# Row sums that come with the adds, squares on ScalarE, and the second FFN's add in two places: a macaron block on one core

## What is computed

```python
x1 = x  + 0.5 * ffn(layernorm(x))           # ffn: one 256x256 matrix, a weighted sum of 8 adapters, and a bias
y  = layernorm(x1)                          # input of the attention block
h  = layernorm(y, ln1_g, ln1_b)             # time-mixed with its predecessor token: xk, xv, xr
ya = y + (sigmoid(xr @ Wr.T) * wkv(xk @ Wk.T, xv @ Wv.T)) @ Wo.T
h  = layernorm(ya, ln2_g, ln2_b)            # mixed again: xck, xcr
kk = square(relu(xck @ Wck.T))
x2 = x1 + ya + sigmoid(xcr @ Wcr.T) * (kk @ Wcv.T)
out = x2 + 0.5 * ffn(layernorm(x2))
# layernorm: m = mean(x), v = mean((x - m)**2), (x - m) / sqrt(v + 1e-5), over the 256 channels
```

## Time and profile before

| | us |
|---|---|
| median of 3 runs (435.98 to 436.53) | 436.53 |
| the profiled execution | 435.98 |
| its span, first to last instruction | 434.2 |
| TensorE's matmuls busy | 419.3 |
| VectorE busy | 380.5 |
| ScalarE busy | 305.9 |
| GpSimd busy | 179.1 |

### The profile page before, as it was taken

The page is one execution under the profiler, slowest core; times in us unless marked ns, Lnnn a source line. Parts: engine busy times, 40 slices in busy tenths (PEclk is TensorE's granted clock), DMA queues, the critical chain, the costliest instruction groups (busy, mean ns, idle before and its releaser), DMA issues. The chain is left out here.

```text
span 434.2 us, 6241 instructions
## 1 busy us (share of the span) xinstructions
PE 419.3 (97%) x2042; PEld 336.1 (77%) x2042; DVE 380.5 (88%) x779; ACT 305.9 (70%) x573; POOL 179.1 (41%) x164
## 2 busy tenths in 40 slices
PE   8989988989999999999999999999999999999996
PEld 8855865668868887798769886888779876988985
DVE  3989989999999999999999999999999999976235
ACT  1158977896689677994789668967797478945420
POOL 1545053626281646344462728154643346033011
PEclk9999999999999999999999999999999999999998
DMA  6991010001000200011000200010001000000101
GB/s 209 385 396 54 2 48 0 2 2 51 0 0 2 97 2 1 0 51 48 2 0 26 74 0 2 0 51 0 2 0 49 2 0 2 30 19 1 49 2 49
DMA packets 15971, 18.52 MB, mean 43 GB/s; under 512 B 1082, under 2 KB 13634, under 8 KB 15938
## 3 DMA queue, kind: packets, MB, share of 16 engines
q1 hardware_dynamic: 14538, 17.05, 11.1%
q10 hardware_dynamic: 1400, 1.07, 0.8%
HBM read 13.92 MB, written 4.19 MB: 42 GB/s over the span
## 5 line engine op out<-in xcount | busy, mean ns | idle before, releaser
L477 PE MATMUL pair<-wcv_sb,kk 128*128 128x256 f32 x448 | 100.4, 380 | 0.0
L477 PEld LDWEIGHTS pair<-wcv_sb,kk 128*128 128x128 f32 x448 | 83.8, 190 | 11.3 <-ACT kk L717 0.6
L1282 POOL TENSOR_TENSOR x2b<-xs,bias_bc 128x512 f32<-128x512 f32 (+1 forms) x16 | 20.1, 1256 | 92.4 <-DVE xs L1100 48.6
L451 PE MATMUL pair<-xck_hi,wck_hi 128*128 128x512 f32 x128 | 54.3, 424 | 0.0
L455 PE MATMUL pair<-xck_lo,wck_hi 128*128 128x512 f32 x128 | 50.6, 395 | 0.0
L452 PE MATMUL pair<-xck_hi,wck_lo 128*128 128x512 f32 x128 | 50.6, 395 | 0.0
L713 ACT ACTIVATE kk<-pair 128x512 f32<-128x512 f32 x64 | 36.4, 591 | 20.0 <-PE pair L455 19.8
L1282 POOL TENSOR_TENSOR x<-x,bias_bc 128x512 f32<-128x512 f32 x14 | 18.1, 1295 | 63.4 <-DVE rwkv L1016 36.3
L1322 POOL TENSOR_TENSOR xs<-x,xa 128x512 f32<-128x512 f32 x16 | 20.4, 1274 | 44.9 <-DVE xa L1022 44.3
L717 ACT ACTIVATE kk<-kk 128x512 f32<-128x512 f32 x64 | 35.9, 626 | 0.0
L1262 POOL TENSOR_TENSOR rstd_x<-vare_x,nhalf 128x4 f32<-128x4 f32 (+2 forms) x26 | 30.1, 1157 | 8.9 <-DVE vare_x L876 7.4
(11 more groups left out here) (159 smaller groups left out, 1069.3 us busy)
## 6 DMA issues: line engine op xcount, KB each, us to landing
x<-in_x_dram SPq DMA_DIRECT2D x8, 512.0 KB, 3.5
out_dram<-xs SPq DMA_DIRECT2D x15, 256.0 KB, 2.1
xt<-in_xt_dram SPq DMA_DIRECT2D x4, 512.0 KB, 7.5
work<-in_ffn_w_dram ACTq DMA_DIRECT2D x4, 256.0 KB, 4.1
work<-in_ffn_w_dram SPq DMA_DIRECT2D x4, 256.0 KB, 4.3
kk<-in_wck_dram SPq DMA_DIRECT2D x1, 1024.0 KB, 10.1
xs<-in_xt_dram SPq DMA_DIRECT2D x2, 512.0 KB, 11.2
wcv_sb<-in_wcv_dram SPq DMA_DIRECT2D x1, 1024.0 KB, 12.9
```

The lines of the kernel that those rows point to most:

```text
L451: nc.tensor.matmul(key_bank(n), wck_hi[:, h, cols], xck_hi[:, h, :], start=h == 0, stop=False)
L477: last = nc.tensor.matmul(bank_of("kv", e, i)[:, t % TB * C:(t % TB + 1) * C], kk[:, n, tok:tok + P], wcv_sb[:, n, :], start=n == 0, stop= ...
L1282: nc.gpsimd.tensor_tensor(dst, tile, bias_bc[:, :].rearrange("p (a c) -> p a c", a=1).broadcast_to([P, tiles, C]), ALU.add).then_inc(done, 1)
```

## The change

Items 0 to 5 (`SUMS_X2`) take x2's statistics, and items from 2 on (`SUMS_X1`) x1's, without bn_stats: the adds that make x1 and x2 on VectorE write each row's sum as well (`accum_out`), for which x2's add becomes one scalar_tensor_tensor for each tile; GpSimd scales the sums (`lower`); ScalarE squares each tile with that as bias, and its accumulator output is the variance (`row_squares`); GpSimd adds epsilon. `add_second(e - 1, 1)` moves behind `add_output(f)`. `stats_x1` goes, for those items, from its place ahead of `norm_output`. The other edits are semaphores, tiles for the sums, and counts.

```diff
+    SUMS_X1 = 2
+    SUMS_X2 = B - 2
...
+            def row_squares(kind, tile, i, t, f):
+                act.wait_ge(lowered_done[kind], i + 1)
+                if t == 0:
+                    act.wait_ge(gated_done, 2 * f + 2)
+                nc.scalar.activation(eb_v[:, t // TB, t % TB * C:(t % TB + 1) * C], tile[:, t, :], ACT.Square, scale=ROOT, bias=lowered[kind][:, t:t + 1],
+                                     accum_out=var_of[kind][:, t:t + 1]).then_inc(var_done[kind], 1)
+
+            def squares_x1(b):
+                for t in range(NT):
+                    row_squares("x1", x1[b % X1], b - SUMS_X1, t, b - 1)
+
+            def squares_x2(e, tiles):
+                for t in tiles:
+                    row_squares("x2", xs[e % XS], e, t, e + 1)
...
                 if e == 0:
                     h1_of(f)
+                if 0 <= e - 1 < SUMS_X2:
+                    squares_x2(e - 1, (0,))
                 key_relu(e, 2)
+                if 0 <= e - 1 < SUMS_X2:
+                    squares_x2(e - 1, (1,))
                 key_relu(e, 3)
...
                 key_square(e, 0)
+                if 0 <= e - 1 < SUMS_X2:
+                    squares_x2(e - 1, (2, 3))
                 if has(f):
                     state_exponentials(f, 0)
...
                 for n in range(HB // 2, HB):
                     key_square(e, n)
+                if has(f + 1):
+                    squares_x1(f + 1)
                 if has(f + 2):
                     stats_x(f + 2)
...
-                        last = nc.vector.scalar_tensor_tensor(tile[:, t, :], product[:, t % TB, :], rstd_x[b % 2][:, t:t + 1],
-                                                              tile[:, t, :], ALU.mult, ALU.add)
+                        last = nc.vector.scalar_tensor_tensor(tile[:, t, :], product[:, t % TB, :], rstd_x[b % 2][:, t:t + 1], tile[:, t, :], ALU.mult, ALU.add,
+                                                              accum_out=sums["x1"][:, t:t + 1] if b >= SUMS_X1 else None)
...
+                    if b >= SUMS_X1:
+                        last = nc.vector.tensor_scalar(normed[:, t, :], x1[b % X1][:, t, :], negm[:, t:t + 1], rboth[:, t:t + 1], ALU.add, ALU.mult)
...
+                if e < SUMS_X2:
+                    for t in range(i * TB, (i + 1) * TB):
+                        last = nc.vector.scalar_tensor_tensor(xs[e % XS][:, t, :], xs[e % XS][:, t, :], 1.0, thc[:, t, :], ALU.mult, ALU.add,
+                                                              accum_out=sums["x2"][:, t:t + 1])
+                    last.then_inc(x2_done, 1)
+                    return
                 nc.vector.tensor_tensor(tok_bank(xs[e % XS], i), tok_bank(xs[e % XS], i), tok_bank(thc, i), ALU.add).then_inc(x2_done, 1)

             def value_stats(e, i):
+                if e < SUMS_X2:
+                    return
...
                 if has(e - 1):
                     add_second(e - 1, 0)
-                    add_second(e - 1, 1)
                 if has(f + 1):
                     add_first(f + 1)
                 if has(f):
                     add_output(f)
-                if has(f + 1):
+                if has(f + 1) and f + 1 < SUMS_X1:
                     stats_x1(f + 1)
+                if has(e - 1):
+                    add_second(e - 1, 1)
                 if has(f):
                     norm_output(f)
...
+            def lower(kind, i, done, count):
+                pool.wait_ge(done, count)
+                nc.gpsimd.tensor_scalar(lowered[kind][:, :], sums[kind][:, :], -ROOT / C, None, ALU.mult).then_inc(lowered_done[kind], 1)
+
+            def add_eps(kind, i):
+                pool.wait_ge(var_done[kind], NT * (i + 1))
+                nc.gpsimd.tensor_scalar(vare[kind][:, :], var_of[kind][:, :], EPS, None, ALU.add).then_inc(vare_done[kind], 1)
...
             def first_inverses(b):
-                pool.wait_ge(vare_done["x1"], b + 1)
                 if b > 0:
                     pool.wait_ge(normed1, 2 * (b - 1) + 2)
                     pool.wait_ge(xa0_done, b)
+                if b >= SUMS_X1:
+                    add_eps("x1", b - SUMS_X1)
+                    nc.gpsimd.tensor_scalar(both[:, :], var_of["x1"][:, :], EPS * EPS / (1.0 + EPS), None, ALU.add).then_inc(both_done, 1)
+                    pool.wait_ge(both_done, b - SUMS_X1 + 1)
+                    nc.gpsimd.tensor_scalar(negm[:, :], sums["x1"][:, :], -1.0 / C, None, ALU.mult).then_inc(negm_done, 1)
+                    inverse_root(rboth[:, :], both[:, :], nhalf[:, :], rboth_done)
...
+                if 0 <= e - 1 < SUMS_X2:
+                    lower("x2", e - 1, x2_done, 2 * (e - 1) + 2)
                 if has(e - 1):
                     bias_to_x2(e - 1, 1)
+                if e - 1 >= SUMS_X2:
                     inverse_std("x2", e - 1)
...
                     hold_exponents(f)
+                if 0 <= e - 1 < SUMS_X2:
+                    add_eps("x2", e - 1)
+                    inverse_std("x2", e - 1)
                 if has(f + 1):

                     pool.wait_ge(aa_done, 2 * f + 2)
                     bias_to_x(f + 1, 0)
                     pool.wait_ge(rwkv_done, 2 * f + 2)
                     bias_to_x(f + 1, 1)
+                if has(f + 1):
+                    lower("x1", f + 1 - SUMS_X1, x1_done, 2 * (f + 1) + 2)
                 if has(f):
                     attention_sum(f, 0)
```

More of the change, by code:

```diff
@@ L106, in build @@
         shift1 = sb("shift1", [P, NT])
+        sums = {k: sb(f"sums_{k}", [P, NT]) for k in ("x1", "x2")}
+        lowered = {k: sb(f"lowered_{k}", [P, NT]) for k in sums}
+        var_of = {k: sb(f"var_of_{k}", [P, NT]) for k in sums}
         mean_x = sb("mean_x", [P, NT])
@@ L174, in build @@
         rstd_done = {k: sem(f"rstd_done_{k}") for k in kinds}
-        rboth_done, negm_done, shift1_done, means_done, vars_done = (
-            sem(n) for n in ("rboth_done", "negm_done", "shift1_done", "means_done", "vars_done"))
+        rboth_done, negm_done, shift1_done, means_done, vars_done, both_done = (
+            sem(n) for n in ("rboth_done", "negm_done", "shift1_done", "means_done", "vars_done", "both_done"))
+        lowered_done, var_done = ({k: sem(f"{n}_{k}") for k in ("x1", "x2")} for n in ("lowered_done", "var_done"))
         xb_first, xb_done, x1_done, normed1, xa0_done, xa2_done, normeda, xs_done, x2_done, x3_done = (
@@ L865, in aggregate @@
             def aggregate(kind, b, tiles=range(NT), part=0):
-                dve.wait_ge(bn_done[kind], b + part + 1)
+                made = (b - SUMS_X2 if kind == "x2" else b) + part + 1
+                dve.wait_ge(bn_done[kind], made)
                 if b > 0 and part == 0:
@@ L871, in aggregate @@
                 last.then_inc(mv_done[kind], 1)
-                dve.wait_ge(mv_done[kind], b + part + 1)
+                dve.wait_ge(mv_done[kind], made)
                 some = slice(tiles[0], tiles[-1] + 1)
@@ L942, in norm_first @@
                 for t in range(NT):
+                    if b >= SUMS_X1:
+                        last = nc.vector.tensor_scalar(normed[:, t, :], x1[b % X1][:, t, :], negm[:, t:t + 1], rboth[:, t:t + 1], ALU.add, ALU.mult)
+                        if t % TB == TB - 1:
+                            last.then_inc(normed1, 1)
+                        continue
                     last = nc.vector.tensor_scalar(normed[:, t, :], x1[b % X1][:, t, :], mv["x1"][:, t, 0:1], rboth[:, t:t + 1], ALU.subtract, ALU.mult)
@@ L1273, in first_inverses @@
                     pool.wait_ge(xa0_done, b)
+                if b >= SUMS_X1:
[4 more added lines that the diff above has]
+                    inverse_root(rboth[:, :], both[:, :], nhalf[:, :], rboth_done)
+                    pool.wait_ge(vare_done["x1"], b + 1)
+                    inverse_root(rstd["x1"][:, :], vare["x1"][:, :], nhalf[:, :], rstd_done["x1"])
+                    pool.wait_ge(rstd_done["x1"], b + 1)
+                    nc.gpsimd.tensor_tensor(shift1[:, :], negm[:, :], rstd["x1"][:, :], ALU.mult).then_inc(shift1_done, 1)
+                    return
+                pool.wait_ge(vare_done["x1"], b + 1)
                 inverse_root(rboth[:, :], both[:, :], nhalf[:, :], rboth_done)
```

## The result

The median fell from 436.47 to 431.68 us (431.02 to 431.75, four runs each), a ratio of 0.9889 with a 95% interval of 0.9874 to 0.9904, which is a gain of 4.2 to 5.5 us. Forecast were 432.4 and a gain of 4.1 us; the range ended at 431.7, 0.02 us above the median measured.

What follows compares the result with a forecast made beforehand. TensorE, 97% busy, was taken as the bound, waiting for VectorE only at L336. Five passes' 3.8 us and the first's 0.40 made 4.2, taken as 4.1: 436.53 - 4.1 = 432.4 us, range 431.7 to 436.8.

Steps and rivals of the forecast that it cites:

- The wait and its size: TensorE waits for VectorE's norm_output only at the transposes L336: 0.80 us in five passes, 0.40 in the first, 4.4 together.
- -0.79 us: On VectorE, two adds of add_second leave their place ahead of xa's variance, which comes 0.79 us sooner.
- +0.44 us: add_first on VectorE meets GpSimd's bias_to_x and is held 0.44 us, between ends of nothing and 1.01.
- Rival 1: Partial gain: GpSimd's hold or the reading of sums costs more, giving 435.2 or 434.7 us; chance 0.20.
- +0.40 us: Four adds of add_first on VectorE now write row sums, taken at 0.10 us each from ScalarE's accumulator read.
- rival 2: Slower: each row sum on VectorE costs more than 0.29 us, giving 437.6 or 441.7 us; chance 0.11.
- The variance: xa's variance on VectorE, ahead of norm_output, was to come at 194.65 instead of 194.60, 0.05 us later.
- The gain of 4.1: At L336, 3.8 us from five passes and 0.40 from the first make 4.2, taken as 4.1 for small late starts.
- the low end: Range's lower limit, 431.7 us: the whole 4.4 us off the median and the scatter of 0.5.
- ScalarE's squares: Eight squares a pass, 0.49 us each, cost nothing if they fit idle time; behind them L345 has 0.33 us margin.
- room, no path: x2's statistics leaving VectorE free about a microsecond, but VectorE next waits there for TensorE's transposed x2.
- rival 3: No change, 436.5 us: the gain is lost at L345 through squares or GpSimd's bias add of x2; chance 0.07.

Runs made afterwards that it cites:

- e2_tail: The changed kernel with its six new small tiles placed behind all others, so the large tiles lie where they lay before: 432.62 us, ratio 0.9896.
- e5: The changed kernel with both halves of add_second ahead of add_first again, as before the change: 431.59 us, ratio 0.9881.
- e6: The kernel before with only the second half of add_second moved behind stats_x1, ahead of norm_output: 438.98 us, ratio 1.0048.
- e7: The changed kernel with each ScalarE square of x2 made twice, the second into a spare tile: 433.74 us, ratio 0.9925.
- e3: The changed kernel with x2's statistics by bn_stats again and x1's by sums: 431.95 us, ratio 0.9883.
- e4: The changed kernel with x1's statistics by bn_stats ahead of norm_output again, x2's by sums, add_second still split: 437.95 us, ratio 1.0025.
- e1: The kernel before with six unused 128x4 tiles ahead of mean_x, so all tiles behind lie 192 bytes further: 436.55 us, ratio 0.9995.
- e8: The changed kernel with two of its six tiles (sums) ahead of mean_x and the other four ahead of xcr_hi: 431.84 us.
- j: The changed kernel with tiles reordered: x2t and xck 64 bytes further than before the change (modulo 256), xcr 192: 431.39 us, ratio 0.9876.
- k: The changed kernel with tiles reordered: x2t and xcr 64 bytes further than before the change (modulo 256), xck 192: 432.07 us.

## Why the prediction missed, point by point

- **The wait and its size** were right: L336 was the only place in the loop where TensorE waited, 4.4 us were to be had, and e2_tail, with the addresses of before, gives 4.4.
- **-0.79 us** for the two adds moved away: right as a term (187.50 to 188.29), though e5 shows that the gain does not need it.
- **+0.44 us** for GpSimd's hold: 0.45 measured (e5 against the changed kernel), 0.46 in e6. Rival 1's "more than half" of GpSimd's instruction over was half: 0.63 of 1.27 us.
- **+0.40 us** for the row sums was mis-sized: 0.04 us, from ScalarE's accumulator read, where VectorE's overlaps the next add. The rule in the Trainium skill, "Vector Engine (DVE) Microarchitecture Reference", section 7, of half throughput with two fp32 SBUF sources and no port for the accumulator's readback does not hold here: 0.41 us a step against 0.40. That was the case of rival 2, slower. The arithmetic with 0.10 us a sum would also have made e5 433.7, and it took 431.59.
- **The variance** came 5.58 us after the output product's start (193.66 - 188.08) instead of 6.03 before (194.60 - 188.57): 0.45 sooner, where 0.05 later was forecast. Of these 0.50 us the mis-sized sums are 0.36. The rest is mostly that rwkv ends sooner against L345's start, by 0.18 us (the next group starts 0.58 ahead of it, at 187.50, before 0.40 ahead): x2's half brings rwkv forward by 0.28, and the faster products bring L345 forward by 0.10.
- **The gain of 4.1** was therefore 0.3 short of 4.4: 0.2 from the sums, and 0.1 taken off for late starts that did not occur.
- **What failed** is the step that the low end rested on, "the whole 4.4 from the median and the scatter": it takes as given that nothing but waits can change for TensorE. The six small tiles were costed at nothing, and their 192 bytes made untouched products 0.8 us faster in all. No row of before could price it, and none of the terms asked where the large tiles go. Without it the changed kernel would take 432.4 us (an estimate: 431.68 and the 0.76 us by which e2's stretch is longer), which is the forecast; that it meets it to a tenth is partly scatter, as the waits gave 4.4 us and not 4.1. e2 itself measured 432.62 where the kernel before took 436.83.
- **The low end as a number** has a slip besides: 436.53 - 4.4 - 0.5 is 431.6, not 431.7, and 431.6 would have taken in 431.68. So it was 0.02 us and a slip that put the result outside, and the traces, not the median, that show the missing term.
- **ScalarE's squares** cost nothing, as said: 0.31 us left before a relu (0.32 forecast), 0.63 before h2 (0.6). Before the exponentials 0.21 is left where 1.44 - 0.98 leaves 0.46: VectorE had become earlier, by the 0.28 us above. e7 shows the cover's end; the margin at L345 was the right thing to watch.
- **x2's half** as "room, no path": right in the changed kernel (e3), but not where VectorE sets the pass (e4). The hold that rival 3 feared from GpSimd's bias add of x2 did occur, VectorE's second mix step waiting behind it:

```profile
207.32 2.45 DVE L999 SCALAR_TENSOR_TENSOR xk<-xr,vec,h 128x512 f32<-128x512 f32 x2
...
206.97 1.59 POOL L1349 TENSOR_TENSOR x2b<-xs,bias_bc 128x512 f32<-128x512 f32 x1
```

The same two mixes in the kernel before:

```profile
209.93 1.41 DVE L961 SCALAR_TENSOR_TENSOR xk<-xr,vec,h 128x512 f32<-128x512 f32 x2
```

They take 2.45 us, 1.04 more than the 1.41 of the kernel before. The room that the missing bn_stats left absorbs it: VectorE reaches the step ahead of these mixes (L990) at 206.12 us, in e3 at 207.45, 1.33 later, and 0.28 of it is left at rwkv.

## What to carry to other kernels

A gain is read from the one wait that it ends, and what fills the gap instead should be shorter than the work of another engine that it covers: that part of the sum held to 0.3 us (4.1 against 4.4). When a change declares new tiles ahead of large ones, ask where the large ones now lie, and compare the steps of untouched products before and after, or put the new tiles last as e2 does, to see the change by itself. A faster product is worth next to nothing while another engine sets the pass: the same 192 bytes gave 0.2 us in e1 and 0.8 us once VectorE no longer held TensorE up.

## What the runs showed of the hardware that I had not expected

- Products of 128x256, each with its own weight load, step by 114 to 120 ns on average, by the byte offset of the tiles in their partition, in a pattern that gave the same times at 0 and 256 bytes, and at 128 and 384 (24 products: 2.74 to 2.88 us). The tiles read by the products just before play a part as well (e8, j, k).
- The accumulator read of VectorE costs about 0.01 us in a sequence of adds, that of ScalarE 0.09.
- GpSimd's bias add holds a VectorE instruction with two SBUF tensors until just before its own end: 0.45 us in `add_first` (to 0.2 us before it), 1.04 in the mixes.
